# First loads of cross attention, rotary, causal attention, ternary feed-forward and sorted rows rewritten in one fp32 program

## The reference, cut to what matters

```
x = x + cross_attention(layernorm(x), ctx)        # layers 0 to 3; 1 and 3 with a key mask
q = q * cos + rotate_half(q) * sin; k likewise    # mixers of layers 0 (heads of 16) and 1 (heads of 64)
tern = clip(round(w / scale), -1, 1); w = w + (tern - w); h = x @ (w * scale).T + gate * (x @ v.T @ fast_b.T @ u.T)
y = (relu(h) ** 2) @ ternary(w_proj).T            # feed-forward of layer 1
out = w2[argmax] @ gelu(w1[argmax] @ x + b1) + b2 # feed-forward of layer 2: one of 14 experts for each token
softmax(causal(q @ k.T) / sqrt(256)) @ v          # mixer of layer 3, one head
```

## Time and profile before

| | us |
|---|---|
| median of 3 runs | 5084.13 (5080.93 to 5087.28) |
| the profiled execution | 5067.95 |
| its span | 5066.2 |

### The profile page before, as it was taken

One profiled execution on the slowest core, in us unless ns is written; L12 is line 12 of the kernel. 1 busy time (PEld: TensorE's weight loads), 2 busy tenths in 40 slices (PEclk: granted clock), 3 DMA queues, 4 the chain that ended last, 5 costly groups with the idle time before them and its releaser, 6 DMA issues. The chain is left out here.

```text
span 5066.2 us, 144787 instructions
## 1 busy us (share of the span) xinstructions
PE 4336.7 (86%) x65818; PEld 3440.2 (68%) x65818; DVE 2436.0 (48%) x4175; ACT 1969.9 (39%) x3858; POOL 569.9 (11%) x274
## 2 busy tenths in 40 slices
PE   6999994599999879999966679999943679999968
PEld 4877773488888668887734357777733568888744
DVE  3555553566666545554544335555524245555521
ACT  3554442233333334444422125544421234444430
POOL 1111101000000021111030011111112021111000
PEclk9999996699999999999987799999976889999979
DMA  2111101021111111111030011111013411111000
GB/s 66 41 35 41 42 16 28 27 73 48 49 50 48 33 63 36 43 39 40 16 84 18 18 50 41 41 35 42 22 24 116 170 58 43 36 42 40 19 19 18
DMA packets 90444, 224.69 MB, mean 44 GB/s; under 512 B 29728, under 2 KB 52768, under 8 KB 87120
## 3 DMA queue, kind: packets, MB, share of 16 engines
q1 hardware_dynamic: 89072, 213.39, 13.5%
q0 software_dynamic: 768, 2.10, 0.1%
HBM read 195.64 MB, written 9.32 MB: 40 GB/s over the span
## 5 line engine op out<-in xcount | busy, mean ns | idle before, releaser
L679 DVE TENSOR_REDUCE x_pm<-banks 128x4 f32<-128x1536 f32 (+2 forms) x512 | 935.4, 1827 | 689.0 <-PE banks L582 689.0
L776 ACT ACTIVATE x_pl<-banks 128x384 f32<-128x384 f32 x1536 | 629.0, 497 | 708.2 <-PE banks L565 708.2
L506 POOL TENSOR_TENSOR x_cl<-xnT,x_ch 128x1601 fp32r<-128x1601 f32 x120 | 400.7, 3339 | 3387.5 <-ACT x_ch L791 3387.5
L781 ACT ACTIVATE x_kT<-banks,x_bk 128x384 f32<-128x384 f32 (+2 forms) x512 | 305.1, 596 | 563.3 <-PE banks L593 563.3
L603 PE MATMUL banks<-x_wh,x_ch 128*128 128x256 f32 (+1 forms) x1664 | 489.8, 294 | 0.0
L593 PE MATMUL banks<-x_ch,x_wh 128*128 128x384 f32 (+2 forms) x1024 | 410.1, 401 | 90.9 <-POOL x_v L513 89.0
L565 PE MATMUL banks<-x_q,x_kT 32*128 32x128 f32 x13312 | 483.7, 276 | 4.4 <-issue 4.2
L582 PE MATMUL banks<-x_kT,x_q 32*128 32x384 f32 (+2 forms) x4096 | 457.1, 511 | 14.2 <-DVE x_v L711 8.9
L603 PE MATMUL banks<-x_wh,x_cl 128*128 128x256 f32 (+1 forms) x1664 | 468.3, 281 | 0.0
L603 PE MATMUL banks<-x_wl,x_ch 128*128 128x256 f32 (+1 forms) x1664 | 467.0, 281 | 0.0
L565 PEld LDWEIGHTS banks<-x_q,x_kT 32*128 32x128 f32 x13312 | 437.0, 185 | 8.9 <-issue 6.3
(11 more groups left out here) (341 smaller groups left out, 6753.4 us busy)
## 6 DMA issues: line engine op xcount, KB each, us to landing
xnT<-in_ctxT SPq DMA_DIRECT2D x120, 800.5 KB, 4.4
e_w<-in_L_pack SPq DMA_DIRECT2D x91, 384.0 KB, 3.1
e_w<-in_L_pack SPq DMA_DIRECT2D x21, 1154.0 KB, 5.6
a_swap<-a_raw SPq DMA_DIRECT2D x64, 128.0 KB
actT<-in_ctxT SPq DMA_DIRECT2D x8, 800.5 KB, 7.5
e_rw<-routed_rows SPq DMA_DIRECT2D x64, 64.0 KB, 2.9
x_rows<-e_zero SPq DMA_DIRECT2D x1, 2688.0 KB, 11.3
e_xt<-x_rows SPq DMA_DIRECT2D x21, 128.0 KB, 5.4
```

Of the source, the lines that this page charges most:

```text
L506: nc.gpsimd.tensor_tensor(cl[:, u, k, 0:CTX], staged(b, k), ch[:, u, k, 0:CTX], ALU.subtract).then_inc(low_done, 1)
L679: nc.vector.tensor_reduce(pm[:, c, :, g], src[:, :, 0:hi - lo], AX.X, ALU.max).then_inc(max_done, 1)
L776: nc.scalar.activation(probabilities(c, j, lo, hi).rearrange("p t q -> p (t q)"), mine[j][:, 0:(hi - lo) * P], ACT.Exp).then_inc(exp_done, 1)
L781: nc.scalar.activation(kT[:, c, lo:hi], mine[1 if g == 0 and inside(b if c else b - 1) else 0][:, 0:hi - lo], ACT.Identity, bias=col[:, c: ...
```

## The change

The pieces of the diff, stage by stage, shortened at "..."; a line in brackets tells in words what stands there.

```diff
+    def load_keys(self, sp, wk):                     # called by refresh after its mask load, ahead of every cross attention
+        sp.dma_start(self.next_w[:], self.dram[wk].rearrange("(c p) n -> p c n", p=P)).then_inc(self.next_in, 16)
+        first = self.narrow[:].rearrange("p c n -> p (c n)")[:, 0:CTX]
+        sp.dma_start(first, self.dram["ctxT"][0, 1]).then_inc(self.next_in, 16)
@@ cross_attention, sync
-            for n, w in enumerate((wk, wv)):
-                sp.dma_start(raw_w[:, n], ...).then_inc(w_in, 16)
             load_context(0, 0)
-            load_context(0, 1)
+            sp.dma_start(raw_v, ...).then_inc(wv_in, 16)
...
-            for k in range(KC):
-                sp.wait_ge(low_done, k + 1)
-                load_context(1, k)
+            sp.wait_ge(low_done, 1)
+            load_context(1, 1)
+            sp.wait_ge(low_done, 2)
+            load_context(1, 0)
@@ gpsimd
-            for k in range(KC):
-                split_low(0, 0, k)
             (memsets of side and v)
+            pool.wait_ge(low_done, 2)
@@ vector
             take_q(0, 0)
             take_q(1, 1)
+            (wl of Wk; cl of the first context, chunk 1, then chunk 0; wl of Wv)
@@ rotary: layer 0, "L0_q", "L0_qr", "L0_k", "L0_kr" with the half-heads of the columns exchanged on the host
+def rotary_computed(net, tag, chunks, wts, outs):
+    UNITS = [(t, c, h) for t in range(2) for c in range(chunks) for h in range(2)]
+            for n, (t, c, h) in enumerate(UNITS):         # tensor: 8 units of 128 x 512
+                for r in range(2):                        # plain and exchanged weights
+                    for k in range(KC):
+                        last = nc.tensor.matmul(net.bank(2 * (n % 4) + r), w[:, 2 * t + r, k, c * P:(c + 1) * P], ...)
+            (vector: two products of PSUM with the tables; gpsimd: one sum of 128 x 512)
@@ rotary_moved (layer 1)
-        part = net.sb(tag + "_part", [P, 2, 2, TOK], ctx=mem)
+        part = net.sb(tag + "_part", [P, RING, 2, TOK], ctx=mem)     # RING = 3
@@ causal_attention
-            with pe.Fori(0, TILES) as t:
+            project(0)                                    # k, q of 512 tokens, from xnT
+            pe.wait_ge(wv_in, 16)
+            for t in range(4):
+                value(t)
+                if t < 2:
+                    score(t)
+            project(1)
+            for t in range(2, TILES):
+                score(t)
+                if t >= 4:
+                    value(t)
+                turn(t - 2)
+                if t >= 3:
+                    attend(t - 3)
+            ...
@@ top1_experts
-    SLOTS = 4
+    SLOTS = 6
+    PART = 7
-        xt = net.sb(tag + "_xt", [P, SLOTS, D], ctx=mem)
+        xt = net.sb(tag + "_xt", [P, TOP1_TILES, D], ctx=mem)
-                    if j >= SLOTS:
-                        sp.dma_start(xt[:, s], x_rows[j * P:(j + 1) * P, :]).then_inc(x_in[s], 16)
+            act.wait_ge(scattered, 16 * TILES)            # on ScalarE's queue
+            for n in range(TOP1_TILES // PART):
+                rows = x_rows[n * PART * P:(n + 1) * PART * P, :].rearrange("(j p) n -> p j n", p=P)
+                act.dma_start(xt[:, n * PART:(n + 1) * PART], rows).then_inc(x_in[n], 16)
@@ ternary, ternary, bit_hidden -> ternary_hidden (one stage)
+    (vector rounds halves: w_fc 0, w_fc 1, w_proj 0, w_proj 1, with one operation over the matrix fewer)
+            def weights(h):                               # tensor: low-rank part and turned weights in one PSUM bank
+                    nc.tensor.matmul(bank, av[:, c * P:(c + 1) * P], uT[:, h * HALF:(h + 1) * HALF], start=True, stop=True)
+                        last = nc.tensor.matmul(bank[:, n * P:(n + 1) * P], q[0][:, t, c * P:(c + 1) * P], net.ident[:],
+                                                start=False, stop=True, skip_group_check=True)
+            weights(0); hidden 0, 1; weights(1); hidden 2 to 11; turn w_proj; hidden 12 to 15     # two matmuls for a hidden tile
+            (scalar: scales the rounded rows, copies the weights, and does both ReLU and Square of each hidden tile)
```

More of the change, by code:

```diff
@@ new lines, in causal_attention @@
+        sc = net.sb(tag + "_s", [P, TILES, P], ctx=mem)
+        negmax = net.sb(tag + "_nm", [P, TILES], ctx=mem)
+        total = net.sb(tag + "_sum", [P, 2, TILES], ctx=mem)
+        pT = net.sb(tag + "_pT", [P, TILES, P], ctx=mem)
+        values = [net.bank(4 + t % 2)[:, 0:D] for t in range(TILES)]
+        scores = [net.bank(6)[:, (t % 4) * P:(t % 4 + 1) * P] for t in range(TILES)]
+        turns = [net.bank(7)[:, (t % 4) * P:(t % 4 + 1) * P] for t in range(TILES)]
+        outs = [net.bank(t % 4)[:, 0:D] for t in range(TILES)]
@@ L1117, in _ @@
         @block.sync
         def _(sp):
[L1119 to L1123, removed]
-            sp.dma_start(mask[:], d["causal"]).then_inc(w_in, 16)
@@ L1181, in _, with take @@
         def _(act):
[L1182 to L1185 removed]
+            def take(h):
+                for i, n in enumerate((1, 0)):
                     for c in range(KC):
[L1187 removed]
+                        m = 2 * i + c
+                        act.wait_ge(qk_full, 4 * h + m + 1)
+                        nc.scalar.activation(qk[:, n, c, h * HALF:(h + 1) * HALF], net.bank(m), ACT.Identity,
@@ L1194, in rank_below @@
+            act.wait_ge(bias_in, 64)
+            take(0)
+            for t in range(2):
+                exponent(t)
+            take(1)
+            for t in range(2, TILES):
+                exponent(t)
 def rank_below(nc, dve, link, gt, eq, vals, tri, rank, n):
@@ new lines, in hidden @@
+            def hidden(n):
+                c, tok = n // 2, slice((n % 2) * HALF, (n % 2 + 1) * HALF)
+                if n >= 4:
+                    pe.wait_ge(relu_done, n - 3)
+                for k in range(KC):
+                    last = nc.tensor.matmul(hidden_bank[n], wfcT[:, k, c * P:(c + 1) * P], net.xnT[:, k, tok], start=(k == 0),
+                                            stop=(k == KC - 1))
+                last.then_inc(made, 1)
+            pe.wait_ge(rank_in, 64)
+            nc.tensor.matmul(net.bank(4)[0:R, 0:D], fbT[:], v[:], start=True, stop=True).then_inc(low, 1)
@@ new lines, in _ @@
+            pe.wait_ge(low_taken, 1)
+            weights(0)
+            pe.wait_ge(wfc_taken, 2)
+            for n in range(2):
+                hidden(n)
+            weights(1)
+            for n in range(2, 8):
+                hidden(n)
+            pe.wait_ge(wfc_taken, 4)
+            for n in range(8, 12):
+                hidden(n)
+            for m in range(4):
+                for c in range(2 * m, 2 * m + 2):
+                    for t in range(2):
+                        pe.wait_ge(pr_ready, t + 1)
+                        at = (c % 2) * D + t * P
+                        last = nc.tensor.transpose(net.bank(m)[:, at:at + P], q[1][:, t, c * P:(c + 1) * P], net.ident[:])
+                last.then_inc(pr_turned, 1)
```

438 lines of the change are left out of this document (261 added, 177 removed).

## The result

The changed kernel takes 4877.65 us, the median of four runs (4868.19 to 4880.05), beside 5082.78 for the kernel before in the same measurement (5080.93 to 5087.28). The ratio is 0.9592 with a 95% interval of 0.9575 to 0.9608. The forecast was 4901, the range 4880 to 4928: faster, as said, but by 23 us more than the forecast and 2 us outside the range.

A forecast was written before the change was run, and what follows sets the result against it. Each edited stage was bound by its own chain, in none by TensorE all through. Gains 49 + 22.8 + 3 + 53.6 + 31 + 23.5, say 183 us, off the median 5084.13 gave 4901 us, range 4880 to 4928.

The forecast's parts named there:

- starts: Starts of the four cross attentions: TensorE begins 8.1 us into each, a gain of 49.7 us, taken as 49.
- rotary of layer 0: Layer 0's rotary stage: 32 matmuls instead of 16 and no DMA, next stage 22.8 us earlier.
- ternary: Joined ternary stage: some 54 us instead of 107.6, a gain of 53.6 us, bounds 50 and 57.
- sorted rows: Sorted rows: scatter costs 5.5 us, first x load 2.2; then 20 tiles at 3.73 us; gain taken as 31 us.
- causal attention: Causal attention stage: 42 us against 65.5, a gain of 23.5 us, with ends at 15 and 28.
- The runs' median, 5084.13, is 16 us above it: Whole program: gain taken off the runs' median instead of the profiled execution's 5067.95 us, giving 4901 us.
- the six staggered turns: Causal attention: turns need 2 us each on TensorE and VectorE, 12 us, then a tail of 4 with the last softmax.
- Rival 2: Sorted rows: the weight stream limits them, price +17 us, 4918 us; chance 0.15.
- the term of 0.25 us a period: Layer 1's rotary: the third slot only removes handovers, 0.25 us for each of 14 periods, 3 us.
- Rival 1: Layer 1's rotary: the third slot pays in full, price -17 us, 4884 us; chance 0.12.
- Rival 3: Cross attention starts: VectorE held by memsets (5.8 us) or first chunk late (up to 15), 4907 to 4916 us; chance 0.15.
- Rival 4: Cross attention: the clock falls and the program is slower than before, at 200 us about 5101; chance 0.02.

The follow-up runs named there:

- experiment 4: The changed kernel once more, no edit, timed beside the kernel before: 4878.31 us, ratio 0.9619.
- experiment 8: The changed kernel with four weight slots instead of six in the sorted rows: 4880.51 us, the stage 144.2 us.
- experiment 6: The changed kernel with the sum of layer 1's rotary on VectorE and GpSimd idle there: 4867.26 us, the stage 74.0 us.

## Why the prediction was right and wrong

The chain of each stage was read rightly in the main: all six groups gained, and the halves add up. As means over all traces of the study that have a part unchanged or changed, the gains are, beside the forecast: starts 45.6 (49), by TensorE's first row; rotary of layer 0 22.2 (22.8); of layer 1 6.2 (3); ternary 53.4 (53.6); sorted rows 177.0 - 139.1 = 37.9 (31); causal attention 68.6 - 37.5 = 31.1 (23.5). The sum is 196 us, against 183 forecast and 196 measured in experiment 4. The miss of 23 us is then some 13 of terms and 10 of the baseline. Either alone would have left the forecast within its range: 4891 with the right baseline, 4888 with the right terms.

**The step that failed first** is "The runs' median, 5084.13, is 16 us above it, and I take the gain off that." Two things are wrong in it. Three runs of one measurement were taken for the middle of a kernel whose executions spread over 37 us; the median of 43, on three chips, is 10 us lower. Why that one measurement stood high stays open (experiment 4). And the gap between the profiled execution and the runs was treated as lying outside the edited stages. Eleven of the 19.5 us between two executions were in stages that the change rewrites, so they had to go into the terms.

**Causal attention** was short by 7.6 us. 2.6 are that draw: 65.5 us was the shortest of three traces. The other 5 are in "the six staggered turns need some 2 us each on TensorE and on VectorE, 12 us, the tail with its last softmax 4". From the last copy of the second projection (4715.12) to the last row added to x (4727.39) it is 12.3 us, not 16: the first row is added after 2.4, four more follow 1.85 us apart, and the last three within 2.5. The turns cost what the forecast said, but the last tiles' softmax is hidden behind the turns of others, and the separate tail of 4 is not there. The projections ahead were 1 to 2 us quicker as well.

**Sorted rows**: 31 was near for that trace (32.4), by luck, since two errors cancel. The first result came 9.7 us later, not 7.7, and the delay lies elsewhere than forecast: the x load was issued 2.3 us later in the stage, where "5.5 us" were meant for the slower scatter, but from its issue to the first turn it took 8.3 us behind the weights, not "2.2 us where 0.3 were needed"; before, it took 2.1 (the two rows below). And the last two intervals are 3.51 and 1.73 us, as they had been before, not 3.73. What the forecast had not seen is the other 5.5 us: in the four traces of the old loop TensorE was granted 0.93, 0.93, 0.89 and 0.86 between the first result and the last, and the stage took 173.1, 173.1, 179.4 and 182.4 us. The changed one is granted 1.00. Length and clock go together there; whether the lower clock made the tiles longer or longer waits lowered the clock, no run separates. The two more weight loads ahead of the first result cost 4.5 us by experiment 8.

```profile
3896.34 1.76 SPq L1536 DMA_DIRECT2D e_xt<-x_rows  x4
3898.43 0.29 PEld L1561 LDWEIGHTS banks<-ident,e_xt 128*128 128x128 f32 x2 [22.78 <-DMA e_xt<-x_rows]
```

Rival 2, the weight stream as the limit, did not happen, though the stream gave 288 GB/s where the forecast asked for 351: with six loads ahead, only 15 remain for 21 tiles.

**Rotary of layer 1**: the mechanism, exclusion, was right and is shown by experiment 6; the term of 0.25 us a period was half of the 0.53 measured (4.95 less 4.42). The two handovers (0.10 and 0.14 us) go, and beside them the first 0.12 to 0.14 us of an operation now runs under the end of the other. Rival 1, the third slot paying in full, fell.

**Starts**: the unmasked ones came at 7.7 and 7.9 us (8.1 forecast), the masked at 10.3. Rival 3 was right for x1 and x3, and its 11.0 us nearly so: VectorE began its chain 6.0 us into the stage (1744.78). The forecast should have had this in its sum; it cost 2.5 us each. In the traces the cast took 2.91 us under a memset and 0.23 without one, the difference 1.82 under a memset and 1.80 without, and the product under GpSimd's sum 3.36 instead of 1.22. The Trainium skill, SBUF — State Buffer, section "SBUF: two separate sides", lets a VectorE operation in a two-port mode, which casts and `tensor_scalar` can be in, and a GpSimd operation lock one another out, and a VectorE operation with two SBUF inputs only against GpSimd operations that read SBUF. The traces agree with both halves; in which mode the cast ran, they do not tell.

**Ternary** took 55.6 us on average where the sum had 54. Its gain agrees only because the old stages took 109.0 on average and not the 107.6 of the one trace. **Layer 0's rotary** took 37.2 where the sum had 37.7. **Rival 4**, a lower clock in cross attention, did not happen: its four stages were granted 0.97, 0.98, 0.97 and 0.98 in the changed kernel and 0.97, 0.97, 0.96 and 0.97 before, and the clock of the whole span rose from some 0.922 to 0.935.

## What to carry to other kernels

Before a gain is taken off a median, compare at least two executions stage by stage: where the change rewrites a stage that differs between them, that stage's spread belongs to the gain. A loop in which TensorE waits in every pass can lose twice, once by the wait and again in the passes that are granted 1.2 GHz; price its dense replacement against the average pass, not the best one. And where GpSimd helps VectorE with data in SBUF, look in the trace whether the two run side by side or hold one another off; in the latter case add both durations, and if VectorE alone is quicker than the sum, as in layer 1's rotary, the help is a loss.

## What the runs showed of the hardware that was not expected

- With two matmuls more per pass, with results that nobody reads, the causal stage took 64.0 us and was granted 0.99 over passes two to eight, in one trace; without them it took 65.5 to 71.2 us, with stretches at 0.50.
- A memset of GpSimd, which reads nothing, stretched VectorE's 128-column cast from 0.23 to 2.91 us in the masked stages and left two-input differences of 1601 columns untouched (1.82 us).
- Under exclusion 0.12 to 0.14 us of each operation still runs under the end of the other: 2.34 + 1.21 + 1.22 us of work took 4.42, not 4.77.
